# Attention layers of a 16-layer network: norm made tile by tile inside the projection stage, other store and load order, heads fetched by ScalarE

## What is computed

```python
def layernorm(x, eps=1e-5):
    m = mean(x, axis=-1); v = var(x, axis=-1)
    return (x - m) / sqrt(v + eps)

h = layernorm(x)
q, k, v = h @ Wq + bq, h @ Wk + bk, h @ Wv + bv      # 16 heads of 8
scores = q @ k.T / sqrt(8)                           # causal, softmax over keys
x = x + (softmax(scores) @ v) @ Wo + bo
```

## Time and profile before

| what | value |
|---|---|
| median of 3 runs | 5766.71 us (5761.96 to 5769.86) |
| the profiled execution's own time | 5796.54 us |
| its span, first to last instruction | 5794.8 us |
| TensorE busy | 4718.3 us, 81% |
| VectorE busy | 3782.7 us, 65% |
| ScalarE busy | 3159.8 us, 55% |
| GpSimd busy | 1685.3 us, 29% |
| mean granted TensorE clock | 0.92 of full speed |

### The profile page before, as it was taken

One profiled execution on the slowest core, in us unless ns is written; L12 is line 12 of the kernel. 1 busy time (PEld: TensorE's weight loads), 2 busy tenths in 40 slices (PEclk: granted clock), 3 DMA queues, 4 the chain that ended last, 5 costly groups with the idle time before them and its releaser, 6 DMA issues. The chain is left out here.

```text
span 5794.8 us, 91401 instructions
## 1 busy us (share of the span) xinstructions
PE 4718.3 (81%) x33501; PEld 2088.3 (36%) x33596; DVE 3782.7 (65%) x4596; ACT 3159.8 (55%) x6002; POOL 1685.3 (29%) x1468
## 2 busy tenths in 40 slices
PE   5677667998679977799766998589877799699999
PEld 2233223443233335333352333256432344233344
DVE  6899657886589943899437992577638710699410
ACT  5666444676448852488524885434466521388621
POOL 0666315885032324322242221000006400123100
PEclk7899888999889988899887999789989999799999
DMA  0000011111021124211242110000000000111100
GB/s 27 0 1 1 4 42 41 42 44 28 10 71 51 51 86 148 71 50 51 83 142 73 49 50 20 6 10 2 5 10 0 20 0 0 37 31 45 42 0 14
DMA packets 132106, 211.55 MB, mean 37 GB/s; under 512 B 36422, under 2 KB 93619, under 8 KB 130293
## 3 DMA queue, kind: packets, MB, share of 16 engines
q1 hardware_dynamic: 126708, 197.74, 11.3%
q0 software_dynamic: 4992, 8.41, 0.5%
HBM read 153.93 MB, written 52.00 MB: 36 GB/s over the span
## 5 line engine op out<-in xcount | busy, mean ns | idle before, releaser
L947 ACT ACTIVATE l_core_probs<-l_core_ps_scores_b 128x512 f32<-128x512 f32 (+3 forms) x3840 | 1610.7, 508 | 581.0 <-PE l_core_ps_scores_b L863 426.2
L1047 DVE TENSOR_REDUCE l_core_chunk_max<-l_core_ps_scores_a 128x2 f32<-128x1024 f32 (+3 forms) x1280 | 1253.7, 1021 | 82.9 <-PE l_core_ps_scores_a L848 47.8
L863 PE MATMUL l_core_ps_scores_b<-l_q_rows_sb,l_k_rows_sb 64*128 64x512 bf16 (+3 forms) x3840 | 944.0, 332 | 32.5 <-ACT l_core_probs L947 10.1
L848 PE MATMUL l_core_ps_scores_a<-l_k_rows_sb,l_q_rows_sb 64*128 64x512 bf16 (+3 forms) x3840 | 741.4, 346 | 163.9 <-DVE l_core_ps_acc L1005 75.9
L996 POOL TENSOR_SCALAR_AFFINE_SELECT l_core_probs<-l_core_probs 128x512 f32<-128x512 f32 x512 | 326.9, 639 | 1169.9 <-ACT l_core_probs L947 1165.7
L878 PE MATMUL l_core_ps_acc<-l_core_probs,l_v 128*9 128x512 f32 (+3 forms) x6144 | 648.9, 494 | 15.9 <-ACT l_core_out_sums L929 9.1
L1047 DVE TENSOR_REDUCE l_core_neg_max<-l_core_ps_scores_a 128x2 f32<-128x256 f32 (+3 forms) x640 | 493.6, 820 | 97.6 <-PE l_core_ps_scores_a L808 96.0
L863 PEld LDWEIGHTS l_core_ps_scores_b<-l_q_rows_sb,l_k_rows_sb 64*128 64x128 bf16 x3840 | 304.4, 94 | 689.9 <-ACT l_core_probs L947 600.4
L1918 POOL TENSOR_TENSOR l_scan_bx<-l_xs,l_scan_b_rows 128x1024 f32<-128x1024 f32 x192 | 452.5, 2357 | 224.1 <-DVE l_scan_states L1928 217.8
L1928 DVE TENSOR_TENSOR_SCAN l_scan_states<-l_scan_ps_decay,l_scan_bx 128x1024 f32<-128x1024 f32 x192 | 439.8, 2290 | 40.7 <-POOL l_scan_bx L1918 15.3
L966 POOL TENSOR_TENSOR l_core_probs_decayed<-l_core_probs,l_decay 128x1536 f32<-128x1536 f32 (+2 forms) x160 | 394.2, 2488 | 156.5 <-ACT l_core_probs L947 156.5
(11 more groups left out here) (323 smaller groups left out, 7683.4 us busy)
## 6 DMA issues: line engine op xcount, KB each, us to landing
l_slots_weights<-m_both_dram SPq DMA_DIRECT2D x78, 512.0 KB
l_q_rows<-l_proj_parts SPq DMA_DIRECT2D x96, 128.0 KB
l_k_rows<-l_proj_parts SPq DMA_DIRECT2D x96, 128.0 KB
l_q_rows_sb<-l_q_rows SPq DMA_DIRECT2D x128, 96.0 KB
l_k_rows_sb<-l_k_rows SPq DMA_DIRECT2D x128, 96.0 KB
l_heads_out<-l_core_out_sums SPq DMA_DIRECT2D x300, 32.0 KB
l_q_rows_sb<-l_q_rows SPq DMA_DIRECT2D x128, 64.0 KB
l_k_rows_sb<-l_k_rows SPq DMA_DIRECT2D x128, 64.0 KB
```

The lines of the kernel that those rows point to most:

```text
L848: mm = nc.tensor.matmul(slot[:, i, 0:w], qs[n % 3][rows, p, qt * P:(qt + 1) * P], ks[n % 3][rows, p, c * NT:c * NT + w], start=True, stop= ...
L863: mm = nc.tensor.matmul(pb[m % 3][:, 0:w], ks[n % 3][rows, p, kt * P:(kt + 1) * P], qs[n % 3][rows, p, q0:q0 + w], start=True, stop=not diag)
L947: nc.scalar.activation(pt[:, ts % RP, j, 0:w], pb[m % 3][:, 0:w], ACT.Exp, scale=scale).then_inc(b_free, 1)
L1047: nc.vector.tensor_reduce(to, pa[e % 2][:, :, 0:width_a(qt, c)], AX.X, ALU.max, negate=True).then_inc(a_free, 1)
```

## The change

Three things change in the attention layers.

- The call of `layer_norm` goes. Centering, variance, roots and the product are written into the projection stage's own lists, one tile at a time, with two buffers in place of four; `centered` uses the PSUM banks that v uses later. TensorE's list takes in iteration t: center(t), variance(t-1), project(t-2). ScalarE's: square(t), root(t-1), and the first and second parts of tile t-3. VectorE's: norm(t-1), and the values of tile t-3 (`turned` in rotary layers, `plain_value` and `plain_third` otherwise). The loads of weights and tables are issued in front of the constants, and TensorE waits for them in front of the first projection.
- SyncE stores batches 0, 1 and 2 as wholes (six DMAs of 1024 tokens each) and batch 3 in two halves. Stack 0 is loaded after the store of batch 1; stack 1 moves to the head of the core's list.
- In the core, ScalarE issues the two DMAs of `heads_back` for batches 0 to 2, in step 6 of head groups 6, 10 and 14. SyncE keeps those of the last batch.

```diff
-        layer_norm(net, tag + "_ln", loads=loads)
+        cen = ps("centered", [P, 2, NT])
+        var = ps("var", [P, 2, NT])
+        pv = cen
...
+                store(0, 0, S, first_stored)
+                store(1, 0, S, stored)
+                sp.wait_ge(first_stored, 16 * 6)
+                load_stack(sp, 0)
+                store(2, 0, S, stored)
+                store(3, 0, NT, stored)
+                store(3, 1, NT, stored)
+                sp.wait_ge(stored, 16 * 24)
...
+                def center(t):
+                    if t >= 2:
+                        pe.wait_ge(xn_ready, t - 1)
+                    nc.tensor.matmul(cen[:, t % 2, :], net.center[:, :], x[:, t * NT:(t + 1) * NT],
+                                     start=True, stop=True).then_inc(cen_ready, 1)
+
+                def variance(t):
+                    pe.wait_ge(sq_ready, t + 1)
+                    if t >= 2:
+                        pe.wait_ge(ln_ready, t - 1)
+                    nc.tensor.matmul(var[:, t % 2, :], net.mean[:, :], sq[:, t % 2, :],
+                                     start=True, stop=True).then_inc(var_ready, 1)
+
+                def project(i):
+                    pe.wait_ge(xn_ready, i + 1)
+                    if i == 0:
+                        pe.wait_ge(loaded, 16 * len(loads))
                     for j in range(2):
                         pe.wait_ge(mm_free, 2 * i + j + 1)
...
+                for t in range(TILES + 2):
+                    if t < TILES:
+                        center(t)
+                    if 1 <= t <= TILES:
+                        variance(t - 1)
+                    if t >= 2:
+                        project(t - 2)
...
+                for t in range(1, TILES + 3):
+                    if t <= TILES:
+                        norm(t - 1)
+                    if t == 3:
+                        dve.wait_ge(loaded, 16 * len(loads))
+                    if t >= 3:
+                        for n in (2 * t - 6, 2 * t - 5):
+                            if rope:
+                                turned(n)
+                                continue
+                            plain_value(n)
+                            if n >= 3:
+                                plain_third(n - 3)
...
+                for t in range(TILES + 3):
+                    if t < TILES:
+                        square(t)
+                    if 1 <= t <= TILES:
+                        root(t - 1)
+                    if t >= 3:
+                        for n in (2 * t - 6, 2 * t - 5):
+                            first(n // 4, n % 4)
+                            if n:
+                                second((n - 1) // 4, (n - 1) % 4)
...
+                load_stack(sp, 1)
                 load_stack(sp, 2)
...
-                    if n >= 4 and n % 4 == 2:
-                        heads_back(n // 4 - 1, HEADS)
...
+                def heads_back(b):
+                    for u in range(2):
+                        act.wait_ge(o_stored[u], 128 * (2 * b + 2))
+                    act.dma_start(o[:, b, :], heads_out[b * P:(b + 1) * P, :]).then_inc(r_in[b], 16)
+                    act.wait_ge(r_out[b], 16)
+                    src = rsums[b * HEADS:(b + 1) * HEADS, :].rearrange("(h o) t -> h o t", o=1)
+                    act.dma_start(r[:, b, :], src.to_broadcast((HEADS, P // HEADS, S))).then_inc(r_in[b], 16)
...
+                    if ts % (4 * NS_) == 2 * NS_ + 6 and ts > 4 * NS_:
+                        heads_back(ts // (4 * NS_) - 1)
```

More of the change, by code:

```diff
@@ L480, in attn_project @@
 def attn_project(net, tag, w, dq, rope, bias, decay, parts, v, qs, ks, load_stack, load_consts_):
-    nc, xn, dram = net.nc, net.xn, net.dram
+    nc, x, xn, dram = net.nc, net.x, net.xn, net.dram
     R = HEADS * dq
@@ L498, in attn_project @@
             loads += [(tab[:, :, :], dram["rope"])]
-        layer_norm(net, tag + "_ln", loads=loads)
         part = sb("parts", [P, 2, 3, T], BF16)
         pq = ps("qk", [P, 4, NT])
-        pv = ps("v", [P, 2, NT])
+        cen = ps("centered", [P, 2, NT])
+        var = ps("var", [P, 2, NT])
+        pv = cen
+        sq, lnv, rstd = (sb(n, [P, 2, NT]) for n in ("squares", "log_var", "rstd"))
+        cen_ready, sq_ready, var_ready, ln_ready, rstd_ready, xn_ready, loaded = (sem(n) for n in (
+            "centered", "squares", "var", "log_var", "rstd", "xn", "loaded"))
         mm_ready, mm_free, v_ready, v_free = (sem(n) for n in ("mm", "mm_free", "v_mm", "v_free"))
@@ L510, in _ @@
             def _(sp):
+                for to, source in loads:
+                    sp.dma_start(to, source).then_inc(loaded, 16)
                 sp.wait_ge(rows_clear, 6)
                 load_consts_(sp)
[L514 to L527, removed]
@@ L528, in _, with store @@
-                sp.wait_ge(stored, 16 * 12 * (B - 1))
+                def store(b, h, width, sem_):
+                    at = b * S + h * NT
+                    done = 4 * b + 2 * h + width // NT * 2
+                    sp.wait_ge(hi, done)
+                    sp.wait_ge(mid, done)
+                    sp.wait_ge(low, done)
+                    for j, n in enumerate("qk"):
+                        for s_ in range(3):
+                            sp.dma_start(parts[n][s_, b * R:(b + 1) * R, h * NT:h * NT + width],
+                                         part[0:R, j, s_, at:at + width]).then_inc(sem_, 16)
@@ L535, in _ @@
                         for m in range(j, NW, 2):
-                            mm = nc.tensor.matmul(pq[:, m, :], ws[m][:, :], xn[:, ds(i * NT, NT)],
+                            mm = nc.tensor.matmul(pq[:, m, :], ws[m][:, :], xn[:, i * NT:(i + 1) * NT],
                                                   start=True, stop=True)
                         mm.then_inc(mm_ready, 1)
+                for t in range(TILES + 2):
[5 more added lines that the diff above has]
+                        project(t - 2)
                 for m in range(T // P):
@@ L572, in plain_third @@
                                             ALU.subtract).then_inc(low, 1)
[L574 to L595, removed]
@@ new lines, in turned @@
+                def turned(n):
+                    h, j = n // 2 % 2, n % 2
+                    dve.wait_ge(mm_ready, n + 1)
+                    dve.wait_ge(t_free, n + 1)
+                    nc.vector.scalar_tensor_tensor(t1[0:R, j, h, :], pq[0:R, j, :], bcol[0:R, j:j + 1],
+                                                   tab[0:R, 0, h * NT:(h + 1) * NT], ALU.add, ALU.mult)
+                    nc.vector.scalar_tensor_tensor(t2[0:R, j, h, :], pq[0:R, 2 + j, :], bcol[0:R, 2 + j:3 + j],
+                                                   tab[0:R, 1, h * NT:(h + 1) * NT], ALU.add, ALU.mult
+                                                   ).then_inc(made, 1)
+                    dve.wait_ge(made, n + 1)
+                    nc.vector.tensor_tensor(t1[0:R, j, h, :], t1[0:R, j, h, :], t2[0:R, j, h, :],
+                                            ALU.add).then_inc(val, 1)
+                    dve.wait_ge(val, n + 1)
+                    dve.sem_inc(mm_free, 1)
@@ new lines, in norm @@
+                def norm(t):
+                    dve.wait_ge(rstd_ready, t + 1)
+                    nc.vector.tensor_tensor(xn[:, t * NT:(t + 1) * NT], cen[:, t % 2, :], rstd[:, t % 2, :],
+                                            ALU.mult).then_inc(xn_ready, 1)
+                for t in range(1, TILES + 3):
[11 more added lines that the diff above has]
+                                plain_third(n - 3)
@@ L596, in _ @@
+                if not rope:
                     for n in range(4 * B - 3, 4 * B):
@@ L624, in second, with square, root @@
                                          ACT.Copy).then_inc(mid, 1)
[L626 to L631, removed]
+                nc.scalar.preload_act_table_set("natural_log_exp_and_others")
+                def square(t):
+                    act.wait_ge(cen_ready, t + 1)
+                    if t >= 2:
+                        act.wait_ge(var_ready, t - 1)
+                    nc.scalar.activation(sq[:, t % 2, :], cen[:, t % 2, :], ACT.Square).then_inc(sq_ready, 1)
+                def root(t):
+                    act.wait_ge(var_ready, t + 1)
+                    if t >= 2:
+                        act.wait_ge(rstd_ready, t - 1)
+                    nc.scalar.activation(lnv[:, t % 2, :], var[:, t % 2, :], ACT.Ln, bias=net.ln_eps).then_inc(ln_ready, 1)
+                    act.wait_ge(ln_ready, t + 1)
+                    if t >= 2:
+                        act.wait_ge(xn_ready, t - 1)
+                    nc.scalar.activation(rstd[:, t % 2, :], lnv[:, t % 2, :], ACT.Exp, scale=-0.5).then_inc(rstd_ready, 1)
+                for t in range(TILES + 3):
[8 more added lines that the diff above has]
+                                second((n - 1) // 4, (n - 1) % 4)
+                second(B - 1, 3)
             @block.gpsimd
@@ L799, in _ @@
                 inverse_rows(B - 1, 12)
```

(2 more changed lines are left out.)

3 lines of the change are left out of this document (1 added, 2 removed).

## The result

The changed kernel takes 5812.1 us (median of 4 runs, 5806.4 to 5821.6) where the kernel before took 5768.3 in runs beside it: a ratio of 1.0079, 95% interval 1.0062 to 1.0097, so 43.8 us or 0.8% slower. The forecast was 5807, +40.5.

A forecast was written before the change was run, and what follows sets the result against it. The prediction took a per-tile cycle through three in-order queues to bound the changed norm-and-projection stretches. Plain -4.6, rotary +40.6 and ScalarE's fetching +4.5 made +40.5 on 5766.7: 5807 us, range 5767 to 5852.

The forecast's parts named there:

- The ring: Norm inside projections: in-order TensorE, ScalarE and VectorE work forms one cycle per tile, 7.4 us plain, 10.9 rotary at full clock.
- The clock: TensorE's idle spells in each cycle lower its granted clock to 0.7 to 0.9, lengthening cycles to 8.5 and 12.3 us.
- The share of 40%: Part of the plain cycle's 2.6 us lower-clock cost that was counted, a little less for rotary.
- Rotary layers: Layers 4 and 6, norm start to core start: 110.9 us each, together 221.8 against 181.2, +40.6.
- the formula: Stretch from norm to core with cycle C: 30.7 + 6C us in plain layers, 37.1 + 6C in rotary ones.
- SyncE in the projections: Fewer stores and stack loads; last stores done 8.7 us after the last third, hidden by 11.0 of v tail and drain.
- The rival with SyncE at the end: Stores still end the projection stage, landings over 8 us: +5 us a layer, 5832 us; chance 0.05.
- Plain layers: Layers 2, 8 and 14, norm start to core start: 81.7 us each, together 245.1 against 249.7, -4.6.
- The core and ScalarE: Attention cores: fetching heads from ScalarE's queue costs 0.3 us for each of 15 pairs, +4.5 us; stack 1's move costs 0.
- full clock: Rival: norm and projection cycles stay at 7.4 and 10.9 us, total 5771, no difference; chance 0.15.
- the lower clock throughout: Rival: all cycles at the lower clock and 1.0 us per pair on ScalarE, about 5876 us; chance 0.08.
- overlap of the queues: Rival: TensorE doesn't hold up the norm, VectorE sets the pace, plain 59.2, rotary 77.6 us, total 5673; chance 0.10.

The follow-up runs named there:

- experiment 3: Changed kernel plus two (plain) or three (rotary) extra f32 matmuls behind the variance of tiles 2 to 7, results unread: ratio 1.002 to the kernel before.
- experiment 5: Changed kernel with stack 0's 14 loads issued right behind batch 0's stores, in front of batch 1's: ratio 1.0044 to the kernel before.
- experiment 1: Changed kernel with VectorE making the values of tile t-3 before the norm of tile t-1: ratio 0.9834 to the kernel before.
- experiment 2: Changed kernel with the layer norm again a separate stage before the projections; stores, stack loads and ScalarE's fetching stay changed: ratio 0.991 to the kernel before.
- experiment 6: Changed kernel with all heads fetched by SyncE's queue again: ratio 1.0095 to the kernel before.
- experiment 8: Changed kernel with values before norm, stack 0's loads early, four centered buffers in plain layers, heads on ScalarE: ratio 0.9793 to the kernel before.
- experiment 9: Changed kernel with values before norm, stack 0's loads early, four centered buffers in plain layers, heads on SyncE: ratio 0.9803 to the kernel before.
- experiment 4: Changed kernel with four centered buffers instead of two and two projection banks, plain layers only: ratio 1.0057 to the kernel before.
- experiment 7: Changed kernel with values before norm on VectorE, stack 0's loads early and heads fetched by SyncE: ratio 0.983 to the kernel before.

## Why the prediction was right

**The ring: right.** The cycle that the prediction built from the earlier trace rows is there, hop by hop: 0.86, 1.06, 0.71, 0.66 and 0.61 where it had 0.86, 1.07, 0.72, 0.66 and 0.75. At full clock it had 7.4 and 10.9 us; experiment 3 gives 6.9 at full clock and 10.6 near it. With the clock as it was, 8.5 and 12.3; the last five intervals of each layer average 8.2 and 11.8. TensorE's idle spell before the first half is 2.9 and 4.4 us, where the prediction had 3.1 and 4.6. One sign was stated wrong: VectorE's wait for the root in layer 4 is 5.8 to 9.3 us in the steady cycles, not 4 to 5; the prediction's own cycle of 12.3, less VectorE's work in it, leaves about 6.4.

**The clock: right in size.** The prediction put 1.1 and 1.4 us a cycle on it, 18 x 1.1 + 12 x 1.4 = 36.6 us; experiment 3 gave back 34.2, with the clock at 0.92 to 1.00. The share of 40% behind the 1.1 was a choice, so the closeness is in part luck. The granted clock of 0.77 to 0.83 between the norms is inside the 0.7 to 0.9 that it named. The Trainium skill, page "TensorE: Matmul & The Clock Gate", section "A second HAM failure mode: psum-queue depth-cycling", has the clock of a bf16 kernel swing where groups of matmuls with short idle spells cycle over banks; these runs in f32 agree, 0.79 with the spells and 0.95 with them filled in layer 4.

**Rotary layers: right.** 110.9 each predicted, 110.0 and 108.0 measured; with the measured cycle of 11.8 the formula would give 107.9, so its other terms were about 1 us too small.

**SyncE in the projections: the step that failed.** The prediction said that the queue "is never 14 transfers behind" and that the v tail hides the last stores. In the rotary layers the tail does hide them: the last store is issued 2.8 and 2.0 us before the last copy of v ends. In the plain layers the third part of a value is made three values after it, so batch 1's last piece is finished one and a half iterations after its value, in the iteration of the last norm, and in layer 2 is stored only from 863.57. The fourteen loads come behind it, while batch 2 becomes ready, so they stand in front of the last 18 stores, and these end the stage. The rival with SyncE at the end (+5 us a layer, chance 0.05) came true in three layers of five, though not by its stated cause, landings over 8 us (3.8 measured): experiment 5, which takes it away, leaves 78.9, 82.8 and 79.4, a mean of 80.4 where the formula has 81.7. What I missed is that "less in the list" is no answer to "what stands in front of the last item when it becomes ready".

**Plain layers** were therefore to gain 4.6 us and lost 7.9. The 12.5 us between them are the loads in front of the stores (14.5, from the last norm to the core), less 2.0 by which the rest of the three layers was overestimated.

**The core and ScalarE: +4.5 predicted, not shown.** The cores grew by 2.7 us in these traces, less than they vary between executions with the same code of the core (2281.2 in experiment 1, 2287.0 in experiment 2). Experiments 6, 8 and 9 find no cost of moving the fetches to ScalarE; 0 would have been the better value for the sum. The reason given for it fails, though: ScalarE's semaphores are not "long passed there", it waits for one at six fetches, and stands idle for 12.4 us in all at twelve (experiment 6). What the prediction put at nothing is the other side, SyncE's fetching: without ScalarE's part the cores are not shorter (2288.3 us in experiment 6 against 2287.7, and 2287.4 in experiment 9 against 2281.9 in 8). The Trainium skill, page "DMA: Bandwidth & Descriptors", section "Issuing engines are not separate DMA queues", promises nothing beyond the issue time from the move; the two pairs agree, with 0.1% and 0.2% between them, inside their intervals.

**The sum.** 36.0 + 4.5 was predicted, 44.7 + 2.7 read from the traces, 43.8 in the medians. Misses on both sides are in it, +12.5 in the plain layers (SyncE) against -3.8 in the rotary layers and -1.8 in the cores: part of the closeness of 5807 and 5812 is cancellation. Of the other rivals, full clock didn't come, nor did the lower clock throughout, and overlap of the queues didn't come, since the written order of three lists forbids it. Experiment 1 shows what the latter would have been: its own price of 5673 stands beside 0.9834 x 5768 = 5672. That is luck in part: it had 59.2 and 77.6 us a layer, where experiment 1 has 62.0, 60.4 and 62.2 and 72.6 and 75.2.

## What to carry to other kernels

Before work is interleaved into a loop, write down for each in-order queue what its iteration waits for and in what order, and look for a ring that goes through all of them; its length is a sum of hops, and busy shares say nothing of it. Then put ready work in front of waiting work on every engine: here two moved lines were worth 2.4%, and buffers only helped behind that. For a queue of transfers, ask what stands in front of the last item at the time when it becomes ready, not how many items are left in all. And take a change of several parts apart: this one held a gain of 53 us and a loss of 98.

## What the runs showed of the hardware

- Work that is thrown away can pay: two or three more f32 matmuls per tile raised the granted clock between the norms from values of 0.77 to 0.83 to values of 0.92 to 1.00, and the kernel ran 34 us faster with them (experiment 3). A matmul of 128x512 f32 starts 0.86 us after the one before it at full clock (two passes of 0.43) and about 1.7 at the lower level, and both are met within one cycle of layer 8.
- A DMA issued by ScalarE took its queue 0.33 us for the heads and 0.55 to 0.87 us for the inverses; the data landed after 3.1 to 4.1 and 4.5 to 6.0 us (changed kernel, 15 of each). In layer 2 the exponentials ran on beside the issues, in the other layers they started 0.5 to 2.1 us late, the most where ScalarE waited between its two DMAs.
- The stages of layer 5 and of layer 7, whose code is the same in all these kernels, took 174 to 180 us each in three traces (the changed kernel, experiments 8 and 9) and 187 to 197 in the eight others, a difference larger than most of the parts measured here. It goes with the time of the kernel before: that one took 5765 and 5768 us beside the first three, 5794 and 5795 beside experiments 1 to 7, and 5797 in its own trace. Its cause was not looked for. Windows of the changed stages are the surer measure.
